# Attention head outputs turned by a VectorE block transpose instead of a copy and four TensorE transposes

## What is computed

```python
scores = jnp.einsum('bhqd,bhkd->bhqk', q, k) * SCALE
attn = jax.nn.softmax(scores, axis=-1)
out = jnp.einsum('bhqk,bhkd->bhqd', attn, v)
return out.transpose(0, 2, 1, 3).reshape(B, Tq, C) @ Wo.T + bo
```

## Time and profile before

| | us |
|---|---|
| median of three runs (lowest, highest) | 4522.98 (4522.26, 4527.35) |
| span of the profiled execution | 4527.3 |
| time of the profiled execution | 4527.35, the highest of the three, if it is the one that the span fits |
| what lies around its span by that | 0.05 |

### The profile page before, as it was taken

How to read it: one execution, slowest core, us unless ns; L and a number is a source line. 1 busy time by engine, 2 the same in 40 slices (tenths; PEclk the granted TensorE clock), 3 DMA queues, 4 the chain that set the end, 5 groups by cost and what they waited for, 6 DMA issues and landing times. The chain is left out here.

```text
span 4527.3 us, 83053 instructions
## 1 busy us (share of the span) xinstructions
PE 3886.3 (86%) x30431; PEld 2824.0 (62%) x30525; DVE 3074.1 (68%) x7110; ACT 2057.9 (45%) x3636; POOL 795.1 (18%) x510
## 2 busy tenths in 40 slices
PE   6799997799377999796399999779997987999899
PEld 5344443798365777575378888635555665555577
DVE  7666664456746666544566666678867887888587
ACT  3355554233103333342044444347775762777510
POOL 6433321401431000000023322410000013000000
PEclk9799999599668999897599999879998998999999
DMA  8233331201311000011054544722210015222000
GB/s 266 86 100 101 101 91 54 68 26 42 125 62 33 19 19 19 28 40 37 13 158 124 132 125 125 230 80 66 66 38 19 1 35 199 60 67 67 28 19 19
DMA packets 234478, 338.02 MB, mean 75 GB/s; under 512 B 39204, under 2 KB 132950, under 8 KB 234167
## 3 DMA queue, kind: packets, MB, share of 16 engines
q1 hardware_dynamic: 218280, 306.66, 21.4%
q0 software_dynamic: 15888, 27.23, 2.8%
HBM read 242.42 MB, written 107.01 MB: 77 GB/s over the span
## 5 line engine op out<-in xcount | busy, mean ns | idle before, releaser
L1918 ACT ACTIVATE a_pT<-a_psS 128x512 f32<-128x512 f32 x1536 | 836.0, 597 | 387.7 <-PE a_psS L1804 382.4
L1990 DVE TENSOR_REDUCE a_mx<-a_psA 128x1 f32<-128x512 f32 x1024 | 656.4, 685 | 82.9 <-PE a_psA L1782 82.8
L1819 PE MATMUL a_psZ<-a_pT,a_V 128*17 128x128 f32 x12288 | 488.8, 278 | 0.0
L1782 PE MATMUL a_psA<-a_ks,a_qs 48*128 48x512 f32 (+1 forms) x1536 | 405.5, 523 | 83.8 <-DVE a_mx L1990 36.9
L1986 DVE CUSTOM_DVE_ANT_0 a_scored<-a_psA,a_hide_q 128x512 bf16<-128x512 f32 x512 | 332.7, 688 | 184.4 <-PE a_psA L1782 183.3
L1819 PEld LDWEIGHTS a_psZ<-a_pT,a_V 128*17 128x17 f32 x12288 | 272.8, 97 | 272.7 <-issue 163.3
L1782 PEld LDWEIGHTS a_psA<-a_ks,a_qs 48*128 48x128 f32 (+1 forms) x1536 | 151.6, 192 | 330.2 <-DVE a_mx L1990 127.7
L1804 PE MATMUL a_psS<-a_qs,a_ks 50*128 50x512 f32 (+1 forms) x1536 | 318.3, 408 | 2.7 <-ACT a_pT L1918 0.8
L3262 DVE SCALAR_TENSOR_TENSOR ex_h<-ex_psU,ex_ub,ex_sg 128x512 f32<-128x512 f32 x129 | 96.9, 751 | 189.3 <-PE ex_psU L159 182.3
L2002 POOL TENSOR_TENSOR X<-X,a_osb 128x512 f32<-128x512 f32 x48 | 61.1, 1278 | 935.3 <-ACT a_osb L1905 917.3
L3208 ACT CAST ex_w_h<-X 128x1024 fp32r<-128x1024 f32 x102 | 106.0, 1040 | 149.5 <-DMA X<-in_L_ffn_gw 145.7
(11 more groups left out here) (606 smaller groups left out, 10227.2 us busy)
## 6 DMA issues: line engine op xcount, KB each, us to landing
a_qs<-a_q_parts SPq DMA_DIRECT2D x576, 64.0 KB, 2.3
a_ks<-a_k_parts SPq DMA_DIRECT2D x576, 64.0 KB, 2.3
a_k_parts<-a_p_kp SPq DMA_DIRECT2D x96, 256.0 KB, 2.6
a_q_parts<-a_p_qp SPq DMA_DIRECT2D x96, 256.0 KB, 3.2
X<-in_L_ffn_gw SPq DMA_DIRECT2D x36, 512.0 KB, 4.4
X<-in_L_ffn_up_w SPq DMA_DIRECT2D x36, 512.0 KB, 3.3
X<-in_L_ffn_down_w SPq DMA_DIRECT2D x36, 512.0 KB, 3.8
top_rows<-blank_rows SPq DMA_DIRECT2D x32, 514.0 KB, 4.8
```

Source lines behind the costliest of these rows:

```text
L1782: nc.tensor.matmul(psA[:, unit(a, par) % 3], qs[r, g % ring, p % 2, q * P:(q + 1) * P], ks[r, g % ring, p % 2], start=True, stop=True).the ...
L1819: last = nc.tensor.matmul(psZ[q * VP:q * VP + VW, g % 2, j * P:(j + 1) * P], V[:, b, kt, g % NG * GH + j, :], pT[:, p % 2, par, kt, q * P: ...
L1918: nc.scalar.activation(pT[:, p % 2, par, kt, :], psS[:, unit(t, par) % 3], ACT.Exp).then_inc(exp_done, 1)
L1990: nc.vector.tensor_reduce(mx[:, p // 2 % 2, par, p % 2, q:q + 1], psA[:, unit(a, par) % 3], AX_X, ALU.max).then_inc(a_used, 1)
```

## The change

ACT's copy and PE's four turns are gone, with the tile `oh` and the entry "heads" of the list. The value products read the queries of pT in another order: matmul q takes queries i*128 + q*32 + c (i of 0..3, c of 0..31), four runs of 32 elements, instead of the 128 queries from q*128. In psZ the 32 rows of quarter q then hold exactly the queries that belong on partitions q*32 to q*32+31, and one transpose of 32x32 blocks by DVE (128x512, PSUM to SBUF, tile `ohT`) brings them there. DVE issues it at the same place as before, the head of its step 8g+13 (`TAKEN` = 5), waiting for the value products alone; reciprocal and multiplication wait for it and read SBUF. PE waits for it (`o_turned`) before it uses that bank again.

```diff
+TAKEN = TB + 1
...
-            found.append((STEPS * g + 12, STEPS * g + 12, "heads", g))
...
+        def tokens_of(x, q):
+            return x.rearrange("p (i q c) -> p q i c", i=TB, q=TB)[:, q]
...
                         if g == 0:
                             pe.wait_ge(z_set, 1)
+                        if g >= 2:
+                            pe.wait_ge(o_turned, g - 1)
...
                             last = nc.tensor.matmul(psZ[q * VP:q * VP + VW, g % 2, j * P:(j + 1) * P], V[:, b, kt, g % NG * GH + j, :],
-                                                    pT[:, p % 2, par, kt, q * P:(q + 1) * P], start=(kt == 0), stop=(kt == TB - 1),
+                                                    tokens_of(pT[:, p % 2, par, kt], q), start=(kt == 0), stop=(kt == TB - 1),
...
+                    if t == first and turned_before(t) > 0:
+                        pe.wait_ge(o_turned, turned_before(t))
...
-                    elif what == "heads":
-                        pe.wait_ge(oh_ready, n + 1)
-                        for j in range(GH):
-                            last = nc.tensor.transpose(ps[:, j * P:(j + 1) * P], oh[:, j, :], G.ident[:])
...
-                        act.wait_ge(o_done, GH * (g + 1))
-                        if g > 0:
-                            act.wait_ge(x_full, number["heads", g - 1] + 1)
-                        nc.scalar.copy(oh[:].rearrange("p j c -> p (j c)"), psZ[:, g % 2]).then_inc(oh_ready, 1)
...
-                    dve.wait_ge(x_full, k + 1)
-                    got = bank_of(k).rearrange("p (j q v) -> p j q v", j=GH, v=VP)
+                    dve.wait_ge(o_done, GH * (g + 1))
+                    if g > 0:
+                        dve.wait_ge(on_ready, g)
+                    nc.vector.transpose(ohT[:].rearrange("p j i v -> p (j i v)"), psZ[:, g % 2]).then_inc(o_turned, 1)
+                    got = ohT[:, :, :, 0:VW]
...
                         link(nc.vector.tensor_tensor(oraw[:], usum[:, u % 2, :, heads, :].rearrange("p q j v -> p j q v"), weight, ALU.mult))
-                        nc.vector.tensor_tensor(oraw[:], oraw[:], got[:, :, :, 0:VW], ALU.add).then_inc(x_free, 1)
+                        dve.wait_ge(o_turned, g + 1)
+                        link(nc.vector.tensor_tensor(oraw[:], oraw[:], got, ALU.add))
...
+                    else:
+                        dve.wait_ge(o_turned, g + 1)
                     nc.vector.reciprocal(rden[:], got[:, :, :, DH]).then_inc(rden_ready, 1)
...
-                    for what, n, k in ending(t - 1, "heads"):
-                        take_output(n, k)
+                    g = t // STEPS - 1
+                    if t % STEPS == TAKEN and 0 <= g < GROUPS:
+                        take_output(g)
```

More of the change, by code:

```diff
@@ L1702, in attention_by_pairs @@
         pT = sb("pT", [P, 2, 2, TB, S])
-        oh = sb("oh", [P, GH, P])
+        ohT = sb("ohT", [P, GH, TB, VP])
         rden, on = sb("rden", [P, GH, TB]), sb("on", [P, 2, TB, D])
@@ L1707, in attention_by_pairs @@
         a_ready, s_ready = [sem("a_ready0"), sem("a_ready1")], [sem("s_ready0"), sem("s_ready1")]
-        a_used, max_ready, exp_done, o_done, oh_ready, rden_ready, x_full, x_free = (
-            sem(n) for n in ("a_used", "max_ready", "exp_done", "o_done", "oh_ready", "rden_ready", "x_full", "x_free"))
+        a_used, max_ready, exp_done, o_done, o_turned, rden_ready, on_ready, x_full, x_free = (
+            sem(n) for n in ("a_used", "max_ready", "exp_done", "o_done", "o_turned", "rden_ready", "on_ready", "x_full", "x_free"))
         if hidden is not None:
@@ L1734, in ending, with turned_before @@
             return [(what, n, k) for k, (_, last, what, n) in enumerate(found) if last == t and what in whats]
+        def tokens_of(x, q):
+            return x.rearrange("p (i q c) -> p q i c", i=TB, q=TB)[:, q]
+        def turned_before(t):
+            return max(0, min(GROUPS, (t - STEPS - TB) // STEPS + 1))
         def bank(t):
@@ L1842, in use @@
                                                     start=(kt == 0), stop=(kt == TB - 1))
-                    elif what == "heads":
-                        pe.wait_ge(oh_ready, n + 1)
-                        for j in range(GH):
-                            last = nc.tensor.transpose(ps[:, j * P:(j + 1) * P], oh[:, j, :], G.ident[:])
                     elif what == "turn":
                         u, k_ = n // KD, n % KD
[L1849 to L1852, removed]
+                        pe.wait_ge(on_ready, NG * (u + 1))
                         for q in range(TB):
@@ L1891, in _ @@
                                 if n >= 4:
-                                    act.wait_ge(x_free, number["heads", n - 4] + 1)
+                                    act.wait_ge(on_ready, n - 3)
                                 nc.scalar.activation(e0[:, n % 4], mx[:, n % 2].rearrange("p r j q -> p (r j) q"), ACT.Exp,
@@ L1896, in _ @@
                             if n >= 2 * TB:
-                                act.wait_ge(x_free, number["heads", NG * (n // TB - 2) + NG - 1] + 1)
+                                act.wait_ge(on_ready, NG * (n // TB - 1))
                             nc.scalar.copy(usum[:, n // TB % 2, n % TB], bank_of(k)[:, 0:H * VW].rearrange("p (h v) -> p h v", h=H)
@@ L1905, in _ @@
                             nc.scalar.copy(osb[:, n % 2], bank_of(k)).then_inc(x_free, 1)
-                    if t >= STEPS + TB and t % STEPS == TB and t // STEPS - 1 < GROUPS:
-                        g = t // STEPS - 1
-                        act.wait_ge(o_done, GH * (g + 1))
-                        if g > 0:
-                            act.wait_ge(x_full, number["heads", g - 1] + 1)
-                        nc.scalar.copy(oh[:].rearrange("p j c -> p (j c)"), psZ[:, g % 2]).then_inc(oh_ready, 1)
                     if 0 <= t < QUARTERS:
@@ L1943, in split_maxima, with take_output @@
                                                    ALU.subtract).then_inc(max_ready, 1)
-                def take_output(g, k):
+                def take_output(g):
                     u, heads = g // NG, slice(g % NG * GH, (g % NG + 1) * GH)
-                    dve.wait_ge(x_full, k + 1)
-                    got = bank_of(k).rearrange("p (j q v) -> p j q v", j=GH, v=VP)
+                    of_heads = on[:, u % 2].rearrange("p i (h d) -> p h i d", h=H)[:, heads]
+                    dve.wait_ge(o_done, GH * (g + 1))
[3 more added lines that the diff above has]
+                    got = ohT[:, :, :, 0:VW]
                     if hidden is not None:
@@ L1952, in take_output @@
                         dve.wait_ge(e0_ready, g + 1)
-                        if g > 0:
-                            dve.wait_ge(rden_ready, g)
                         weight = e0[:, g % 4].unsqueeze(3).to_broadcast([P, GH, TB, VW])
                         link(nc.vector.tensor_tensor(oraw[:], usum[:, u % 2, :, heads, :].rearrange("p q j v -> p j q v"), weight, ALU.mult))
-                        nc.vector.tensor_tensor(oraw[:], oraw[:], got[:, :, :, 0:VW], ALU.add).then_inc(x_free, 1)
[L1958 to L1962, removed]
+                        dve.wait_ge(o_turned, g + 1)
+                        link(nc.vector.tensor_tensor(oraw[:], oraw[:], got, ALU.add))
+                        got = oraw[:]
+                    else:
+                        dve.wait_ge(o_turned, g + 1)
                     nc.vector.reciprocal(rden[:], got[:, :, :, DH]).then_inc(rden_ready, 1)
                     dve.wait_ge(rden_ready, g + 1)
-                    nc.vector.tensor_tensor(on[:, u % 2].rearrange("p q (h d) -> p h q d", h=H)[:, heads], got[:, :, :, 0:DH],
-                                            rden[:].unsqueeze(3).to_broadcast([P, GH, TB, DH]), ALU.mult).then_inc(x_free, 1)
+                    nc.vector.tensor_tensor(of_heads, got[:, :, :, 0:DH], rden[:].unsqueeze(3).to_broadcast([P, GH, TB, DH]), ALU.mult
+                                            ).then_inc(on_ready, 1)
                 for t in steps:
```

## The result

The changed kernel takes **4595.95 us** (median of 4 runs, 4594.98 to 4611.63) against 4525.16 of the kernel before on the same chip (4 runs): ratio 1.0159, interval 1.0141 to 1.0177. Forecast were 4569.4 (4543 to 4592): +46 where the runs have +71. The profiled execution is the slowest of the four (span 4609.9), so stretches in it are some 16 us worse than in the median run.

What follows compares the result with a forecast made beforehand. DVE's maxima were taken to set the pace in layers 2 and 3, and DVE's burst behind an output to delay PE in layer 0. 33.6 + 17.4 - 4.6 = +46.4 us gave 4569.4 us, range 4543 to 4592.

Steps and rivals of the forecast that it cites:

- The transpose, layers 2 and 3: Groups with maxima: DVE's added 0.69 us transpose delays the reciprocal 0.58 us in 58 groups, +33.6 us.
- The four turns, removed: PE's 0.66 us of turns per output: hidden behind its wait for DVE, so removal gains nothing.
- PE idle longer: Sign of being right: PE idles longer before the maxima of the step after the output, in layer 0 too.
- Layer 0: Groups with maxima: the transpose delays DVE's next reading and PE's load 0.60 us in 29 groups, +17.4 us.
- The ends: Ends of the three attentions, without maxima, where ACT sets the step: 1.5 us gained a layer, -4.6 us.
- Strided reads: Value products reading four runs of 32 elements instead of one of 128: taken to cost nothing.
- copy: ACT's removed copy of 0.59 us: hidden by ACT's own idle time while maxima run, so no gain there.
- renamed waits: PE's wait for a transpose before reusing the bank, and ACT's and DVE's waits for earlier groups: nothing.
- The mean of 286 ns for a value product: Sign of being right: the value products' mean stays unchanged at 278 ns.
- layer 0 doesn't hide the transpose: Rival denied here: layer 0 hides the transpose and gains 8.4 us instead of losing 17.4; 4543.6 us, chance 8%.
- it isn't two passes: Rival denied here: DVE's transpose costs two passes, 1.22 us, or several instructions; +46 us more, 4616, chance 6%.
- the reads aren't slower: Rival denied here: strided reads slow the value products, up to 49 us for each tenth; 4618 us, chance 4%.

Runs made afterwards that it cites:

- run 1: Changed kernel plus four idle TensorE turns in layers 2 and 3, in PE's step while DVE takes the output; 4565.95 us, ratio 1.0072 to the kernel before.
- Run 4: Kernel before, copy and turns kept, with an added DVE block transpose ahead of each output in layers 2 and 3 alone; 4563.43 us, ratio 1.0075.
- run 3: Kernel before, copy and turns kept, with an added DVE block transpose ahead of each output in all three layers; 4598.28 us, ratio 1.0136.
- run 2: Kernel before with only the strided order of queries in the value products, copy and turns kept; 4527.86 us, ratio 0.9986.
- run 5: Changed kernel with POOL instead of DVE multiplying by the reciprocals in layers 2 and 3; 4547.20 us, ratio 1.0045 to the kernel before.
- run 6: Changed kernel plus one idle TensorE turn in layers 2 and 3, in PE's step while DVE takes the output; 4575.08 us, ratio 1.0099 to the kernel before.
- runs 1 and 7: The second of these: changed kernel plus four idle TensorE turns in layers 2 and 3, two steps earlier, ahead of the block transpose; 4611.35 us, ratio 1.0172.

## Why the prediction was wrong

**The transpose, layers 2 and 3: right.** The transpose takes 0.708 us for 0.69, and a regular group of the changed kernel 0.56 more for 0.58. Once the clock is held (run 1), a layer takes 14.9 and 15.1 more, ends included, for 15.3; some 0.8 of that is run 1's own, as its added turns lengthen the ends (the last three intervals take 30.04 us for 29.25). Run 4, with turns and no gain at the ends, has 17.4.

**The four turns, removed: the step that failed.** "Hidden, so its removal gives nothing" counted the turns only as time that PE could save. But they were also work that PE did just ahead of its wait for DVE. Without them, and with DVE's work 0.6 longer, PE's load stands idle 1.55 us instead of 0.47, and the clock falls in some of the groups: 22.8 and 14.6 us in layers 2 and 3 of the profiled execution (against run 1), 30 in the medians (4596 against 4566). That term stood at nothing. The prediction listed "PE idle longer" as a sign that it was right, and no rival priced it. The missed question is what else an engine loses when its idle time grows.

**Layer 0: too high.** Forecast 0.60 in a group with maxima, 17.4; measured 0.42 (539.8 against 528.1 over 28 groups), 10.3 for the layer with its end. PE and DVE around an output, to set beside the earlier trace rows:

```profile
390.28 0.08 DVE L1987 DVE_READ_ACCUMULATOR2_ANT a_mx<- 128x1 f32 x1
390.28 0.71 DVE L1950 STREAM_TRANSPOSE a_ohT<-a_psZ 128x512 f32<-128x512 f32 x1
390.92 0.40 DVE L1957 TENSOR_TENSOR a_oraw<-a_usum,a_e 128x272 f32<-128x272 f32 x1
...
393.20 0.19 PEld L1790 LDWEIGHTS a_psA<-a_ks,a_qs 48*128 48x128 f32 x2 [1.19 <-DVE a_mx L1987]
```

The transpose starts together with the accumulator's read and not behind it. So the independent operation comes 0.64 behind the start of that read, where it came 0.17 behind it before: 0.47 later, not 0.60, and it takes 0.40 for 0.44. In run 3 the transpose starts 0.17 behind that read, and a group costs 0.59 more. The wait of PE's load of 0.47 became 1.19, and the clock stayed at 1.00 (240 to 740 us): this wait, with 0.70 of idle time between PE's matmuls, doesn't lower it there.

**The ends: right.** The last three intervals of layer 3 sum to 29.25 us for 30.77, so -1.5, as forecast from the earlier trace rows.

**Strided reads, copy, renamed waits at nothing: right** for the reads (run 2); the other two have no run of their own, and the sum below leaves nothing for them. The mean of 286 ns for a value product, which the prediction wanted unchanged, is the clock's doing: the median stays at 273, as before, and run 1, with the same reads, has a mean of 277.

**The sum.** Layers 0, 2 and 3 add 10.2 + 14.9 + 15.1 = 40.2 us by run 1, where 46.4 were forecast; the clock adds the 30, and the two make some 70 of the 71 measured. That the layer 0 term was 7 too high made the miss smaller; this is luck. Of the rivals none came: layer 0 doesn't hide the transpose, it isn't two passes, the reads aren't slower.

**Open** is why only some groups lower the clock, though all have the same wait, and where the border lies: by PE's load run 5 waits 1.23 and has no long interval, run 6 waits 1.20 and has four. By the idle time of the matmuls (0.93 and 1.02) the two are in order, but one profiled execution of each is no proof.

## What to carry to other kernels

Before work is taken off an engine that "has time anyway", ask what fills its wait afterwards: TensorE's clock is a price of idle time, and the granted clock by stretches shows it where busy shares don't. If the wait must be, leave or put matmuls into it: here four turns in the wait kept the clock up, and the same four two steps earlier didn't. And work moved to the engine that sets the pace costs most of its duration (0.56 of 0.71 us here), however little the others then have to do: the better version here took work off DVE.

## What was not expected of the hardware

- Waits of 1.55 us once in 11.9 lower the granted clock at places from 1.00 to 0.50, though PE is busy some 90% of the stretch; filled with four 128x128 turns (run 1) they don't. The Trainium skill (TensorE: Matmul & The Clock Gate, What's actually happening) has the clock throttled by default and released by activity; the runs agree, and show that it counts how the activity lies in time (runs 1 and 7 do the same work and have no long interval and 6).
- A DVE multiplication of two SBUF inputs took 3.9 us instead of 0.42 when it began 0.02 behind a POOL operation of 5.37 us. The Trainium skill (SBUF — State Buffer, SBUF: two separate sides) says that such a pair excludes each other for the whole instruction of the first. The trace agrees in part: the multiplication ends 1.45 before POOL's row does. The operation at 333.60, two SBUF inputs too, kept its 0.40 beside the POOL operation in front, but it began 0.98 before the end of that row, so both would fit if the exclusion ended over 1.4 before POOL's row does. That is not shown: POOL's spans in the profile are rough, and no run here tried another phase.
- Four runs of 32 elements in place of one of 128 as moving operand cost nothing (277 against 278 ns for a value product, run 2).
